# Shared first products on four banks, a halved last q·k product, LN3 statistics on ScalarE and earlier loads at the transition, in a linear-attention and mixture-of-experts layer

## What is computed

```python
y  = ln(x)
xn = LN1(y)
q, k, v = xn @ wq + bq, xn @ wk + bk, xn @ wv + bv     # per token: 16 heads x 16
fq, fk = elu(q) + 1, elu(k) + 1
s = einsum("nhd,ngd->nhg", fq, fk)                     # within one token, over its heads
attn = (s @ v) / (s.sum(-1) + 1e-6)
a  = y + attn @ wo + bo
x1 = x + a + gelu(LN2(a) @ fc_w + fc_b) @ proj_w + proj_b
z  = ln(x1)                                            # LN3
shared = (silu(z @ sg_gate.T) * (z @ sg_up.T)) @ sg_down.T
top two of 8 experts by z @ gate_w.T, softmax weights of the two
routed = sum over both of weight * (silu(z @ wg[e].T) * (z @ wu[e].T)) @ w_down[e].T
out = x1 + shared + routed
```

## Time and profile before

| | us |
|---|---|
| median of 3 runs (1786.31 to 1788.27) | 1786.4 |
| profiled execution, whole time | 1787.39 |
| its span, first to last instruction | 1785.3 |
| mean granted TensorE clock in the span | 0.977 |

### The profile page before, as it was taken

The page is one execution under the profiler, slowest core; times in us unless marked ns, Lnnn a source line. Parts: engine busy times, 40 slices in busy tenths (PEclk is TensorE's granted clock), DMA queues, the critical chain, the costliest instruction groups (busy, mean ns, idle before and its releaser), DMA issues.

```text
span 1785.3 us, 25208 instructions
## 1 busy us (share of the span) xinstructions
PE 1662.2 (93%) x7115; PEld 1203.4 (67%) x7161; DVE 1212.4 (68%) x2117; ACT 805.2 (45%) x1837; POOL 1190.9 (67%) x668
## 2 busy tenths in 40 slices
PE   2588999999999999999999998989999999999997
PEld 1354665665665665566566565668888888888886
DVE  7999999999999999999999996132222222222221
ACT  4255556556565465465465454323232323223232
POOL 4978889899898898898898893224333333433333
PEclk8798999999999999999999999989999999999999
DMA  5102112111111112112112112066777767777774
GB/s 201 47 13 71 48 40 57 48 34 50 59 29 53 56 27 59 47 35 59 48 35 60 48 25 60 25 188 158 156 166 154 169 152 166 157 157 164 155 169 77
DMA packets 89455, 157.19 MB, mean 88 GB/s; under 512 B 8896, under 2 KB 72128, under 8 KB 89024
## 3 DMA queue, kind: packets, MB, share of 16 engines
q1 hardware_dynamic: 60512, 112.58, 20.4%
q0 software_dynamic: 28896, 44.06, 14.6%
HBM read 101.79 MB, written 48.56 MB: 84 GB/s over the span
## 4 chain that ended last, share of the span: by engine, by line
PE 56%; DVE 20%; POOL 12%; issue 8%; ACT 3%; DMA 1%; POOLq 0%; SPq 0%; DVEq 0%; ACTq 0%
PE p_b L1502 10%; PE p_b L1513 10%; PE p_q L1502 7%; PE p_b L1332 7%; PE p_b L1379 6%; PE p_b L1445 5%; DVE p_q L931 5%; POOL prod_pool L496 4%; DVE prod L922 4%; DVE prod L945 4%; PE p_v L1502 3%; POOL prod_pool L510 2%; DVE qkv L958 2%; PE p_q L1304 2%; POOL prod_pool L517 2%
## 5 line engine op out<-in xcount | busy, mean ns | idle before, releaser
L611 POOL DMA_INDIRECT out_rows<-prod_pool,prod x142 | 220.7, 1554 | 383.6 <-ACT prod_pool L849 353.3
L496 POOL TENSOR_TENSOR prod_pool<-prod_pool 128x2048 f32<-128x2048 f32 (+2 forms) x192 | 370.7, 1931 | 15.1
L1379 PE MATMUL p_b<-bT,fc_sb 128*128 128x512 f32 x512 | 230.4, 604 | 1.3 <-ACT bT L781 1.3
L1332 PE MATMUL p_b<-proj_sb,hid 128*128 128x256 f32 x1024 | 230.5, 379 | 0.0
L1332 PEld LDWEIGHTS p_b<-proj_sb,hid 128*128 128x128 f32 x1024 | 189.6, 190 | 29.4 <-issue 0.5
L931 DVE TENSOR_REDUCE p_q<-prod 128x128 f32<-128x2048 f32 (+1 forms) x64 | 189.3, 2957 | 1.2
L922 DVE TENSOR_TENSOR prod<-p_q,eqk 128x4096 f32<-128x4096 f32 (+1 forms) x48 | 186.8, 3891 | 4.8 <-DVE attn L971 0.3
L945 DVE TENSOR_TENSOR prod<-p_q,v_dve 128x4096 f32<-128x4096 f32 (+1 forms) x48 | 186.8, 3891 | 1.6
L958 DVE TENSOR_REDUCE qkv<-prod 128x256 f32<-128x4096 f32 (+1 forms) x48 | 186.6, 3887 | 1.6
L1502 PE MATMUL p_b<-prod,exp_up 128*128 128x256 f32 x840 | 187.1, 379 | 0.0
L1445 PE MATMUL p_b<-x3T,sgup_sb 128*128 128x512 f32 x384 | 177.5, 601 | 6.4 <-issue 5.5
(11 more groups left out here) (179 smaller groups left out, 2880.7 us busy)
## 6 DMA issues: line engine op xcount, KB each, us to landing
exp_up<-in_experts SPq DMA_DIRECT2D x71, 768.0 KB
prod<-rows_sorted SPq DMA_DIRECT2D x71, 260.0 KB
xin<-in_x SPq DMA_DIRECT2D x16, 512.0 KB, 3.4
xres<-in_x SPq DMA_DIRECT2D x16, 512.0 KB, 3.7
xres<-xmid POOLq DMA_DIRECT2D x16, 512.0 KB, 4.6
out_rows<-x SPq DMA_DIRECT2D x16, 512.0 KB, 2.9
exp_dn<-in_experts SPq DMA_DIRECT2D x8, 384.0 KB, 5.1
out_rows<-prod_pool,prod POOLq DMA_INDIRECT x142, 3.8
```

The lines of the kernel that those rows point to most:

```text
L496: done(g.tensor_tensor(prod_pool[:, at:at + n * w], prod_pool[:, at:at + n * w], prod_pool[:, at + n * w:at + 2 * n * w], ALU.add))
L611: pool.indirect_dma_start(out=out[:, :], out_offset=bass.IndirectOffsetOnAxis(ap=tok_i[j][:, a:a + 1], axis=0), in_=yg[j][:, a * D:(a + 1) ...
L1332: ins = t_.matmul(o, src[:, k, t * P:(t + 1) * P], w[:, k, :], start=k == 0, stop=bias_at is None and k == chunks - 1)
L1379: ins = t_.matmul(bnk[:], fc_sb[:, k, f * P:(f + 1) * P], bT[:, k, :], start=k == 0, stop=k == KC - 1)
```

## The change

1. `shared_bank` becomes p_b2, p_b3, p_b0, p_b1, p_b2, p_b3. On PE, parts 0 and 1 come before the projection u = 1, parts 2 and 3 behind it. Part 2 waits for the first half of the residual, part 3 for the second, parts 4 and 5 for the first and second copy of ACT.
2. `products_2(c, 3)` is done in two halves of 8 heads; `residual_2(c, j, 1)` stands between them. p_q1 is freed behind the second half.
3. The statistics of LN3 go from DVE to ACT, in two halves (`ln3_scales`); x1_read counts every half of the residual. In the calls with `more`, ACT does them between `take_qkv(c+1, 0)` and `take_qkv(c+1, 1)`; in call 15 behind the last `take_shared`, in call 16 before the Silu table.
4. The token numbers of a block are moved on by ACT (`token_numbers`) instead of POOL.
5. In call 17 the ranks stand between the halves of `down`. `gate_last` multiplies in three pieces as they are copied.
6. SP issues expert weights 0 and 1 before it waits for pads and scatters, then row tiles 0 and 1. PE does `gate_up(0, 0)` before the transposes of tile 1.

```diff
-        shared_bank = (p_b2, p_b3, p_b0, p_b2, p_b3, p_b2)
+        shared_bank = (p_b2, p_b3, p_b0, p_b1, p_b2, p_b3)
...
-                    wait(sp, x1_read, c - 1)
+                    wait(sp, x1_read, 2 * (c - 1))
...
             sp.wait_ge(tables_ready, 1)
+            load_up(0, 0)
+            load_up(1, 1)
             sp.wait_ge(pads_stored, 16 * EXPERTS)
             sp.wait_ge(scattered, 16 * 2 * TPB * BLOCKS)
...
             load(0, 0)
-            load_up(0, 0)
             load(1, 1)
-            load_up(1, 1)
...
             def scatter(c, j):
+                wait(pool, tok_written, c - 1)
                 wait(pool, slots_ready, c - 1)
-                stand_alone(pool)
-                done(g.tensor_scalar(tok[:], tok[:], float(BLOCK), None, ALU.add))
-                stand_alone(pool)
-                done(g.tensor_copy(rows[j % 2][:, :, C_TOK], tok[:]))
                 stand_alone(pool)
...
-            def scales_3(c):
-                wait(act, x1_read, c)
-                a.activation(sq_c[:], mv_c[:, :, 1], ACT.Ln, bias=eps_1[:, 0:1]).then_inc(ln3_log, 1)
-                act.wait_ge(ln3_log, c)
+            def ln3_scales(c, j, k):
+                tiles = range(TPB // 2 * k, TPB // 2 * (k + 1))
+                half, n = slice(tiles[0], tiles[-1] + 1), 2 * (c - 1) + k + 1
+                wait(act, x1_read, n)
+                for t in tiles:
+                    a.activation(act_junk[:, t, :], x1[(j + 1) % 2][:, t, :], ACT.Copy, accum_out=sum_c[:, t:t + 1]
+                                 ).then_inc(ln3_sum, 1)
+                act.wait_ge(ln3_sum, TPB // 2 * n)
+                a.activation(mean_c[:, half], sum_c[:, half], ACT.Copy, scale=-1.0 / D).then_inc(ln3_mean, 1)
+                act.wait_ge(ln3_mean, n)
+                for t in tiles:
+                    a.activation(act_junk[:, t, :], x1[(j + 1) % 2][:, t, :], ACT.Square, bias=mean_c[:, t:t + 1],
+                                 accum_out=square_c[:, t:t + 1]).then_inc(ln3_var, 1)
+                act.wait_ge(ln3_var, TPB // 2 * n)
+                a.activation(sq_c[:, half], square_c[:, half], ACT.Ln, bias=eps_1[:, 0:1], scale=1.0 / D
+                             ).then_inc(ln3_log, 1)
+                act.wait_ge(ln3_log, n)
                 wait(act, rows_ready, TPB * (c - 1))
-                a.activation(rs_c[:, 0, :], sq_c[:], ACT.Exp, scale=-0.5).then_inc(ln3_std, 1)
+                a.activation(rs_c[:, 0, half], sq_c[:, half], ACT.Exp, scale=-0.5).then_inc(ln3_std, 1)
+                act.wait_ge(ln3_std, n)
+                for t in tiles:
+                    a.activation(rs_c[:, 1, t:t + 1], rs_c[:, 0, t:t + 1], ACT.Copy, scale=mean_c[:, t:t + 1]
+                                 ).then_inc(ln3_scale, 1)
...
+            def token_numbers(c, j):
+                a.activation(tok[:], tok[:], ACT.Identity, bias=block_1[:, 0:1]).then_inc(tok_moved, 1)
+                act.wait_ge(tok_moved, c - 1)
+                a.activation(rows[j % 2][:, :, C_TOK], tok[:], ACT.Copy).then_inc(tok_written, 1)
...
                     keep_scales(c)
+                if stage_c:
+                    token_numbers(c, j)
...
                     take_qkv(c + 1, 0)
+                if stage_b and (more or not core):
+                    ln3_scales(c, j, 0)
+                    ln3_scales(c, j, 1)
+                if more:
                     take_qkv(c + 1, 1)
-                if stage_b:
-                    scales_3(c)
...
                     take_shared(c, range(4, 2 * HCH))
+                if core and not more:
+                    table_exp_ln()
+                    ln3_scales(c, j, 0)
+                    ln3_scales(c, j, 1)
...
-                done(v.tensor_tensor(flat[:, 512 * k:512 * k + 512],
-                                     res[:, 512 * k:512 * k + 512], (p_b0, p_b1)[k][:], ALU.add))
-                for t in range(TPB // 2 * k, TPB // 2 * (k + 1)):
-                    done.later(v.bn_stats(st6[:, t, :], x1_b[:, t, :]))
-                if k == 1:
-                    averages(mv_c)
-                    dve.sem_inc(x1_read, 1)
+                v.tensor_tensor(flat[:, 512 * k:512 * k + 512], res[:, 512 * k:512 * k + 512], (p_b0, p_b1)[k][:],
+                                ALU.add).then_inc(x1_read, 1)
...
-                    products_2(c, 3, True)
+                    products_2(c, 3, False, 0, half)
                 if stage_b:
                     residual_2(c, j, 1)
                 if core:
+                    products_2(c, 3, True, half, HEADS)
...
-                if stage_b:
-                    shift_3(c)
...
-                announce(dve, v.tensor_tensor(sg_g[:], sg_g[:], sg_u[:], ALU.mult), shared_h, BLOCKS)
+                for i in range(HCH):
+                    wait(dve, up_taken, 2 * HCH * (BLOCKS - 1) + 2 * (i + 1))
+                    ins = v.tensor_tensor(sg_g[:, i, :], sg_g[:, i, :], sg_u[:, i, :], ALU.mult)
...
-                    wait(pe, up_taken, 2 * HCH * (c - 3) + 3)
+                    wait(pe, up_taken, 2 * HCH * (c - 3) + 4)
                     transpose_block(attn, (p_b0, p_b1), attnT_psum)
...
-                    down(c, range(TPB - 1 if stage_b else TPB))
+                    down(c, range(TPB - 1 if stage_b else TPB // 2 if stage_c else TPB))
+                if stage_c and not stage_b:
+                    ranks(c)
+                    down(c, range(TPB // 2, TPB))
...
                 if stage_c and stage_b:
-                    shared_up(c, range(1))
+                    shared_up(c, range(2))
                 if more:
                     project_x(c + 1, 1, "P")
                 if stage_c and stage_b:
-                    shared_up(c, range(1, 4))
+                    shared_up(c, range(2, 4))
...
-                    if three and n == 2:
-                        wait(pe, x1_read, c)
-                    if n >= 2:
-                        earlier = {2: 0, 3: 1, 4: 2, 5: 4}[n] if three else n - 1
-                        wait(pe, up_taken, 2 * HCH * (c - 2) + earlier)
+                    if three and n in (2, 3):
+                        wait(pe, x1_read, 2 * c - 3 + n)
+                    elif n >= 2:
+                        wait(pe, up_taken, 2 * HCH * (c - 2) + n - (3 if three else 1))
...
             gT(0, 0)
+            gate_up(0, 0)
             gT(1, 1)
-            gate_up(0, 0)
```

More of the change, by code:

```diff
@@ L62 @@
 ORDER = (POOL_TILE, 0, 1, 2)
-POOL_STEPS = 16
+POOL_STEPS = 14
 HH = HEADS * HD
@@ L455, in load_up @@
                              ).then_inc(up_loaded[j], 16)
+            sp.wait_ge(pads_at, 1)
+            sp.wait_ge(init_stored, 48)
+            for e in range(EXPERTS):
+                row = sp.value_load(pad_at[0:1, e:e + 1], min_val=0, max_val=EXPERTS * REGION - TILE)
+                sp.dma_start(rows_sorted[bass.ds(row, TILE), :],
+                             rows_sorted[EXPERTS * REGION:EXPERTS * REGION + TILE, :]).then_inc(pads_stored, 16)
+            sp.wait_ge(tables_ready, 1)
+            load_up(0, 0)
+            load_up(1, 1)
+            sp.wait_ge(pads_stored, 16 * EXPERTS)
+            sp.wait_ge(scattered, 16 * 2 * TPB * BLOCKS)
             load(0, 0)
-            load_up(0, 0)
             load(1, 1)
-            load_up(1, 1)
             store(BLOCKS + 1, BLOCKS + 1)
@@ L1173, in _ @@
             done(v.memset(eps_1[:], EPS))
+            done(v.memset(block_1[:], float(BLOCK)))
             done(v.memset(eps_2[:], EPS * EPS))
```

48 lines of the change are left out of this document (21 added, 27 removed).

## The result

| | before | after |
|---|---|---|
| median, us | 1787.2 | 1761.3 |
| its runs, us | 1786.31 to 1788.27 (4) | 1759.67 to 1761.95 (4) |
| span of the profiled execution, us | 1785.3 | 1759.8 |
| ratio, 95% interval | | 0.9854 (0.9837 to 0.9871) |

The forecast was 1760.0 (1752 to 1771), faster. The span of the profiled execution is 25.5 us shorter, against 26.4 forecast. Two terms of the sum are each off by more than that difference, in opposite directions.

The account below looks back on a forecast made before the run. TensorE, 93% busy, was taken to bound the kernel, waiting mainly for VectorE to free p_q1. Terms -19.0 - 3.5 + 0.3 + 2.4 - 6.6 = -26.4 us gave span 1758.9, median 1760.0 us, range 1752 to 1771.

Parts of the forecast that it names:

- The wait for p_q1: 13 steady periods: 19.0 of TensorE's 20.0 us wait go, and 3.5 us lost to a reused bank; periods 66.1 to 66.4.
- That is a tie: Steady periods: p_q1 comes free 0.15 us later, TensorE asks 1.72 us later, against a wait of 1.54 us.
- the 1.0 us kept back: Steady periods: 1.0 us over all periods left as remaining wait, for rounds where VectorE is last.
- LN3 on ScalarE at no cost: Steady periods: LN3's statistics take ScalarE 3.3 us per half and cost nothing, with 1.9 us of cover.
- The cover of 2.4 us: Steady periods: ScalarE's LN3 may run 1.9 + 0.5 us longer; each us beyond costs 13.
- GpSimd 0.3 us from binding: Steady periods: GpSimd's gate product is in time for TensorE's `down` by 0.3 us or somewhat more.
- Rival (b): Steady periods: GpSimd binds, its loop 66.8 us against TensorE's 66.1, 8 us in all, 1768 us; chance 0.12.
- Block 1 (+0.3): Block 1: VectorE waits 2.6 us inside the product pair, so what it saved is gone; +0.3 us.
- Block 15 (+2.4): Block 15: LN3 behind the last shared copy delays wo 0.5 us, low clock behind adds 1.9; bounds -0.5 and +4.
- VectorE's wait for wo: Sign of being right: VectorE waits over 2.5 us for wo, against 1.11 us before.
- The table load: Block 15, ScalarE: priced at 1.28 us from the trace, against about 2.66 us with a drain by the Trainium skill.
- The transition (-6.6): Before the experts: earlier ranks, scatter and row loads start the first expert product sooner; -6.6 us, bounds 0 and -8.

Follow-up runs that it names:

- experiment 1: Kernel after with only the order put back (one shared part ahead of the second projection, three behind): 1783.1 us, ratio to the kernel before 0.9979.
- experiment 2: Kernel after with only the first shared products put back on three banks, new order kept: 1784.8 us, ratio to the kernel before 0.9983.
- experiment 8: Kernel after with twelve unused Squares a period (3.8 us) added on ScalarE within the LN3 statistics: 1786.5 us, ratio to the kernel before 0.9992.
- experiment 4: Kernel after with LN3's statistics back on VectorE and the last q·k product whole, new order and banks kept: 1807.4 us, ratio to before 1.0111.
- experiment 5: Kernel after with only the token numbers put back from ScalarE to GpSimd: 1769.3 us, ratio to the kernel before 0.9899.
- experiment 6: Kernel after with the last q·k product run whole, then the second residual half: 1759.5 us, ratio to the kernel before 0.9846.
- experiment 7: Kernel after with block 15's LN3 statistics moved ahead of its Silu table and shared copies: 1754.6 us, ratio to the kernel before 0.9818.
- experiment 10: Kernel after with SyncE's old load order (row, weight, row, weight, all behind the waits for pads and scatter): 1760.1 us, ratio to before 0.9846.
- experiment 3: Kernel after with only LN3's statistics back on VectorE, averages and shift included, scales on ScalarE: 1797.5 us, ratio to the kernel before 1.0057.
- experiment 12: Kernel after with block 15's LN3 ahead of its Silu table and the last q·k product whole except in block 15: 1752.0 us, ratio to before 0.9799.
- experiment 9: Kernel after with two of the transition's eight pads issued by ScalarE, six by SyncE: 1759.2 us, ratio to the kernel before 0.9841.

## Why the prediction was right, and where it was off

- **The wait for p_q1 (-19.0 and -3.5).** Right in cause: experiments 1 and 2 give back what order and banks took. Too small: 13 periods gave 26.9 us, 2.07 each, where I took 1.73, and the period of 65.89 us lies below the 66.1 to 66.4 that I named as a sign. I priced a stop at its shown idle time. Experiment 1 shows 0.2 us more for each: the last matmuls ahead of it run out (1.88 us where the next starts after 1.72) and the first behind it are longer (1.96 against 1.88, the same rows). With the 1.54, the 0.27 and 0.24 for that, a period comes to 2.05.
- **"That is a tie" and the 1.0 us kept back.** The free came 6.22 us after the first residual half, 0.13 earlier than before (6.35, from 806.39 to 812.74), not 0.15 later: a residual of 0.69 takes a step of 0.60. The tie went to TensorE, by 0.27 us. Nothing had to be kept back.
- **LN3 on ScalarE at no cost.** Right: 3.3 us per half, 2.19 us of idle behind it. The cover of 2.4 us was an underestimate: in the undisturbed periods of experiment 8, 3.2 us of the dose are hidden.
- **GpSimd 0.3 us from binding.** Right, 0.33; experiments 4 and 5 show what each side of it costs. Rival (b) was priced at 8 us, and experiment 5, a realisation of it, lost 8. That is partly luck: 0.42 us a period, 5 us in 12, is GpSimd's, and the rest is one fall of the clock and what lies outside these periods. That the rival has a second price, the clock behind the router's products, I had not seen.
- **Block 1 (+0.3).** Measured +0.25, with VectorE's wait of 2.65 us inside the pair as worked out (2.6). Against the kernel before the transposes came 1.0 us later, 0.6 of which stood there before the block's own work. What I did not ask is what the whole product would do here: it is 2.2 us faster (experiment 6).
- **Block 15 (+2.4).** Measured +3.4. wo came as worked out (+0.2, against +0.5), and so did the low clock behind it (+1.5, against +1.9); it fell a second time, in the `down` products, +1.7, which I had not counted. Experiment 7 confirms that the place of LN3 opened the stop.
- **VectorE's wait for wo.** Forecast above 2.5 us as a sign, measured 1.39 (1.11 before). The 2.4 us that VectorE sheds between its first residual and the next block's products do not all show as idle time, since wo itself now comes 2.1 us earlier.
- **The table load.** 1.28 us, and LN3's first operation follows at once (1062.45 and 1063.74 on ScalarE). The Trainium skill (ScalarE: Activation LUTs, What ACT_TABLE_LOAD costs) puts a drain of about 1380 ns behind every switch of sets; none shows here.
- **The transition (-6.6).** Too large: -4.3 at the first expert product, -2.4 two tiles on. The step that failed is "the last scatter starts 4.0 us before ..., row load 0 goes at 1176.8". Counted from the first MLP product of call 16, the row load goes 2.4 us earlier and not 4.0. Two terms of it were wrong. The half of the `down` products that now stands behind the ranks was taken as about 3.3 us; it is 2.6, because the low clock is in the first half (12 products in 4.54 us, then 12 in 2.84). And the 0.7 us of part 4 help the scatter but not the eight pads, 1.36 us each to issue and 4.9 to land, and in the kernel after these are the last that SyncE waits for. The row load that I let follow the weights freely gained nothing by them either (experiment 10). Worse than worked out as well: the wait of 3.31 us brought the low clock onto 16 products (6.10 us, where I had counted on less than the 5.57 of before).

The sum was right by luck in part, because 4.4 us too little in the steady part met 5.3 us too much in block 15 (1.0) and the transition with the tiles behind it (4.3).

## What to carry to other kernels

Where one engine's wait is removed, work out what each part of the change is needed for against the next engine's slack: here order, bank and the moved statistics are worth their 25 us only together (each taken back alone costs 22 us or more), while the split product and the early weight loads are worth nothing that shows here, or less. A stop of TensorE costs more than its idle time: here 0.2 us at the projections, and 1.6 to 3 us more when the clock fell behind it. It fell in most periods at the `down` products of experiment 4 and in 2 of 12 at the projections of experiment 3, so look at single periods: a mean clock of 1.00 over hundreds of us can hide a fall. At the edges of a pipeline (first and last block) an order tuned for the steady state is often the wrong one; by the medians 9 of the 35 us between the kernel before and the best one lay there.

## What the runs showed that I had not expected

- In these runs the low clock went by the place of a wait more than by its length. Behind the router's 16 products it came after waits of 1.6 to 1.9 us in 10 of 12 periods (experiment 4), and after 0.34 us once (experiment 5); at p_q1 after 2.2 to 2.6 us in 2 of 12 (experiment 3), and after 1.4 to 1.8 us never (experiment 1). Behind one and the same stop of 2.7 us it came in one execution (experiment 12) and not in another (experiment 7). What decides it was not tried.
- A direct DMA whose address is read from a table costs SyncE 1.36 us each for eight of them (10.88 us), of which the issue row itself shows 0.53.
- A scatter's last transfer took 7.8 us with two 768 KB weight loads started beside it (experiment 9), against 3.77 in the kernel before, which starts none there.
